# Cross-attention on one core: the turned probabilities moved on two DMA queues, and two score tiles in pairs of 64 rows

## The reference

```python
# B = 8, C1 = C2 = 512, N = 1024, D = 64
q = einsum('bcn,dc->bnd', x1, Wq) + bq
k = einsum('bcn,dc->bdn', x2, Wk) + bk[:, None]
v = einsum('bcn,dc->bdn', x2, Wv) + bv[:, None]
attn = softmax(einsum('bnd,bdm->bnm', q, k), axis=2)
out = einsum('bcm,bnm->bcn', v, attn) + x1
```

## Time and profile before

| | |
|---|---|
| runs | 634.26, 635.60, 635.65 us; median 635.6 |
| profiled execution | 635.0 us, span 633.2 us |
| mean granted TensorE clock | 1.000 |
| TensorE busy | 629.5 us (99%) |
| VectorE, ScalarE, GpSimd busy | 442.9, 328.2, 143.3 us |
| DMA | 102.05 MB, mean 161 GB/s |
| issues of `pt_raw<-blocks` | 240, all on SyncE's queue, 2.3 us each to landing |

### The profile page before, as it was taken

The page is one execution under the profiler, slowest core; times in us unless marked ns, Lnnn a source line. Parts: engine busy times, 40 slices in busy tenths (PEclk is TensorE's granted clock), DMA queues, the critical chain, the costliest instruction groups (busy, mean ns, idle before and its releaser), DMA issues.

```text
span 633.2 us, 13435 instructions
## 1 busy us (share of the span) xinstructions
PE 629.5 (99%) x5318; PEld 590.1 (93%) x5318; DVE 442.9 (70%) x511; ACT 328.2 (52%) x430; POOL 143.3 (23%) x115
## 2 busy tenths in 40 slices
PE   9999999999999999999999999999999999999998
PEld 7888899999999999999999999999999999999986
DVE  6995768847778477794777947778568776597351
ACT  6786535735457345474454653555626547265120
POOL 0332200631007400083000830016300353004100
PEclk9999999999999999999999999999999999999999
DMA  8633426963269532776328762287533974345442
GB/s 334 215 133 83 128 84 181 331 143 111 73 176 324 133 126 82 187 285 166 99 83 204 281 159 89 100 227 260 137 93 114 248 243 114 99 132 133 109 145 81
DMA packets 42758, 102.05 MB, mean 161 GB/s; under 512 B 8176, under 2 KB 10224, under 8 KB 42736
## 3 DMA queue, kind: packets, MB, share of 16 engines
q1 hardware_dynamic: 42736, 101.75, 53.4%
HBM read 51.64 MB, written 16.78 MB: 108 GB/s over the span
## 4 chain that ended last, share of the span: by engine, by line
PE 94%; ACT 2%; SPq 2%; DMA 1%; DVE 1%; issue 0%
PE acc_ps L1158 48%; PE acc_ps L1115 23%; PE s_ps L1080 5%; PE s_ps L1228 4%; PE s_ps L1215 3%; PE acc_ps L1178 3%; PE acc_ps L1353 2%; SPq L298 2%; PE acc_ps L1338 1%; PE s_ps L1082 1%; ACT pt_raw L546 1%; PE acc_ps L1190 1%; PE s_ps L1329 1%; DMA pt_raw<-in_front_dram 1%; ACT pt_raw L552 0%; ACT xs_hi L465 0%
## 5 line engine op out<-in xcount | busy, mean ns | idle before, releaser
L1158 PE MATMUL acc_ps<-pt_hi,vt_hi 64*128 64x512 f32 x960 | 201.5, 386 | 0.2 <-DVE pt_lo L727 0.2
L1158 PE MATMUL acc_ps<-pt_lo,vt_hi 64*128 64x512 f32 x960 | 201.3, 386 | 0.0
L1158 PE MATMUL acc_ps<-pt_hi,vt_lo 64*128 64x512 f32 x960 | 201.3, 386 | 0.0
L1158 PEld LDWEIGHTS acc_ps<-pt_hi,vt_hi 64*128 64x128 f32 x960 | 104.3, 184 | 6.5 <-issue 0.8
L1158 PEld LDWEIGHTS acc_ps<-pt_lo,vt_hi 64*128 64x128 f32 x960 | 104.3, 184 | 5.8
L1158 PEld LDWEIGHTS acc_ps<-pt_hi,vt_lo 64*128 64x128 f32 x960 | 104.3, 184 | 5.8
L1115 PE MATMUL acc_ps<-wv_lo,xs_hi 64*128 64x512 f32 x448 | 95.8, 390 | 0.0
L1115 PE MATMUL acc_ps<-wv_hi,xs_hi 64*128 64x512 f32 x448 | 94.9, 386 | 0.0
L433 POOL TENSOR_TENSOR vt_lo<-vt_lo,v_part 128x64 fp32r<-128x64 f32 x56 | 21.0, 380 | 322.1 <-DVE vt_lo L727 322.1
L558 ACT ACTIVATE probs<-s_ps,negmax 128x1024 f32<-128x1024 f32 x56 | 62.5, 1117 | 54.9 <-DVE negmax L814 54.4
L814 DVE TENSOR_REDUCE negmax<-s_ps 128x1 f32<-128x1024 f32 x64 | 76.7, 1210 | 19.7 <-PE s_ps L1082 18.9
(11 more groups left out here) (140 smaller groups left out, 879.2 us busy)
## 6 DMA issues: line engine op xcount, KB each, us to landing
pt_raw<-blocks SPq DMA_DIRECT2D x240, 128.0 KB, 2.3
stage<-in_x_dram SPq DMA_DIRECT2D x32, 512.0 KB, 6.3
o_sb<-in_x_dram SPq DMA_DIRECT2D x64, 256.0 KB, 3.1
out_dram<-o_sb SPq DMA_DIRECT2D x63, 256.0 KB, 2.1
stage<-in_ctx_dram SPq DMA_DIRECT2D x28, 512.0 KB, 9.0
pt_raw<-in_front_dram SPq DMA_DIRECT2D x4, 512.0 KB, 5.7
v_part<-sums SPq DMA_DIRECT2D x56, 32.0 KB, 1.8
stage<-in_front_dram SPq DMA_DIRECT2D x2, 512.0 KB, 7.6
```

Of the source, the lines that this page charges most:

```text
L1158: mm = nc.tensor.matmul(acc_ps[:, OUT_BANK[group], :], v[rows, m, group * P:(group + 1) * P], p[rows, m, :], start=(swap == 0 and m == 0 a ...
```

## The change

Two things are changed. First, `move` is split: SyncE issues the transfers of steps 0 and 1, ScalarE those of steps 2 and 3, eight each. ScalarE's `move(b, 0)` stands at the head of `v_phase(b)`, its `move(b, 1)` behind the roundings of the next x in `batch(b)`. Both wait for `s_blk` as SyncE's do. Second, score tiles 2 and 3 of the first batch are made by `scores_rows`. For this GpSimd copies columns 256 to 511 of Q's high and low part to `q_dup`, and TensorE waits for the copies.

```diff
+SP_STEPS = (0, 1)
+ACT_STEPS = (2, 3)
...
@@ sync, move
                 sp.wait_ge(s_blk, half_of(b, h) * NT + NT)
-                for step in range(NQ):
+                for step in SP_STEPS:
                     for i in range(NQ):
                         j = (i + step) % NQ
                         sp.dma_start(pt_raw[j * Q:(j + 1) * Q, i, :, :],
...
@@ gpsimd
             pool.wait_ge(s_qlo_a, 1)
             first_x1_lo_b(2)
             first_x1_lo_b(3)
+            pool.wait_ge(s_x1lo_e, 2)
+            pool.wait_ge(s_x1lo_o, 2)
+            pool.wait_ge(s_qhi_a, 1)
+            nc.gpsimd.tensor_copy(q_dup[D:2 * D, QH:NH], q_st[0:D, QH:NH].bitcast(F32)).then_inc(s_qdup_a, 1)
+            pool.wait_ge(s_qdup_a, 1)
+            nc.gpsimd.tensor_copy(q_dup[0:D, QH:NH], q_st[D:2 * D, QH:NH].bitcast(F32)).then_inc(s_qdup_a, 1)
+            pool.wait_ge(s_qdup_a, 2)
...
@@ scalar
+            def move(b, h):
+
+                act.wait_ge(s_blk, half_of(b, h) * NT + NT)
+                for step in ACT_STEPS:
+                    for i in range(NQ):
+                        j = (i + step) % NQ
+                        nc.scalar.dma_start(pt_raw[j * Q:(j + 1) * Q, i, :, :],
+                                     blocks[i * Q:(i + 1) * Q, j, :, :, :].rearrange("p m t r -> p m (t r)")
+                                     ).then_inc(s_moved, 16)
+
             def v_phase(b):
+                move(b, 0)
                 exp(b, 4)
                 exp(b, 5)
...
                         round_x1(nb, 3)
+                move(b, 1)
                 if not last:
                     q_cross(nb, first)
...
@@ tensor
-            scores_next(0, 2)
-            scores_next(0, 3)
+            pe.wait_ge(s_qdup_a, 2)
+            scores_next_rows(0, 2)
+            scores_next_rows(0, 3)
```

More of the change, by code:

```diff
@@ L214, in build @@
         s_acc = sem("s_acc")
+        s_qdup_a = sem("s_qdup_a")
         s_qdup_b = sem("s_qdup_b")
@@ L1102, in scores_next_rows @@
                 scores_rows(t)
-            def scores_next(b, t):
-                pe.wait_ge(s_exp, b * ST + t - 1)
-                scores(t)
             def v_rows(m, swap, k):
```

## The result

| | before | after |
|---|---|---|
| median | 634.86 us (634.26 to 635.65, 5 runs) | 675.11 us (672.63 to 676.14, 5 runs) |
| ratio, with 95% interval | | 1.0623 [1.0598, 1.0648] |
| profiled execution, span | 635.0 us, 633.2 us | 676.1 us, 674.3 us |
| mean granted TensorE clock | 1.000 | 0.974 |

The account below looks back on a forecast made before the run. TensorE, busy 629.5 of 633.2 us, was taken as the bound. From 635.0 us, +5.1 (ScalarE's issues), -0.33 (SyncE's relief) and 0 (score tiles) gave 639.8, raised to 640.1 us; range 634.4 to 652.

Parts of the forecast that it names:

- What bounds the kernel: TensorE, busy 629.5 of 633.2 us; another engine matters only where it is late for TensorE.
- Part 1: First batch's score tiles 2 and 3: two slots saved, 0.45 us, turn into a wait for VectorE's sum; 0 us.
- the bound of 29.9: First batch: GpSimd's two copies to `q_dup`, priced as twice-as-wide ones, end at 29.9, before TensorE wants them at 30.62.
- Part 2: SyncE makes 8 issues, not 16; last rows land about 5 us earlier, batch 0's `pt_lo` gap goes: 0.33 us gained once.
- part 3: ScalarE's eight issues ahead of exp(4) make score tile 6 0.73 us late, seven times: +5.1 us; `move(b, 1)` is free.
- the price of an issue: ScalarE's issues priced by SyncE's same transfer, 0.591 us, pitch 0.63 us: eight take 5.0 us.
- Rival B: Two queues hinder each other; in full, one issue shuts out the other, tile 6 5.8 us late, 680 us; chance 0.22.
- partial form: Queues hinder each other about half as much: pitch 0.9, stall 2.9 us, 655 us; half of the 0.22.
- Rival A: ScalarE's issues are cheap, pitch 0.37, all hidden ahead of tile 6: 634.7 us, or 634.2; chance 0.23.

Follow-up runs that it names:

- the kernel with the same target: Against the kernel after, ScalarE's source order became 2, 3, 0, 1: nth transfers read opposite halves, write the same target block; 656.1 us, ratio 1.0351.
- the kernel with opposite halves: Against the kernel after, SyncE moves source blocks 0 and 1, ScalarE 2 and 3: nth transfers read and write opposite halves; 648.5 us, ratio 1.0211.

## Why the prediction was wrong, step by step

**What bounds the kernel**: right. TensorE does, and only where another engine is late for it. All of the loss is in the matmul starts.

**Part 1, the tiles, 0 us**: right. VectorE's sum and the turn behind it in the kernel after, and GpSimd's two copies:

```profile
28.00 0.39 POOL L419 CAST q_dup<-q_st 64x256 fp32r<-64x256 f32 x1
28.46 0.40 POOL L421 CAST q_dup<-q_st 64x256 fp32r<-64x256 f32 x1
...
31.46 0.74 DVE L763 SCALAR_TENSOR_TENSOR sums<-acc_ps,bias_q,sums 64x512 f32<-64x512 f32 x1 [0.43 <-ACT sums L475]
...
32.35 1.07 PE L1340 MATMUL acc_ps<-ident,blocks 128*128 128x128 f32 x8 [0.16 <-DVE sums L763]
```

The copies end at 28.86, a us ahead of the bound of 29.9. The turn starts behind the sum, 0.15 us after its end, as before; it starts 0.18 us earlier, as the last Q product does (30.21 against 30.39). From start to start less a slot TensorE waits 0.33 us where about 0.4 was forecast; the 0.16 in the row counts from the end that the profile gives the last score matmul.

**Part 2 and batch 0, -0.33 us**: wrong, +2.2 us and a stretch of low clock. The prediction reckoned ScalarE's issues of this `move(0, 1)` at 5.0 us, 55.14 to 60.2, 0.3 us late for `q_cross`. ScalarE in the kernel after, then VectorE and TensorE:

```profile
54.96 7.81 ACTq L600 DMA_DIRECT2D pt_raw<-blocks  x8
62.81 1.02 ACT L475 ACTIVATE sums<-s_ps 64x1024 f32<-64x1024 f32 x1 [8.30 <-issue]
...
69.15 3.88 ACT L475 ACTIVATE pt_hi<-pt_raw 128x1024 fp32r<-128x1024 f32 x4
...
70.85 4.62 DVE L749 TENSOR_TENSOR pt_lo<-pt_raw,pt_hi 128x1024 fp32r<-128x1024 f32 x4
...
72.21 0.50 PE L1175 MATMUL acc_ps<-pt_hi,vt_hi 64*128 64x512 f32 x2 [2.31 <-DVE pt_lo L749]
```

`q_cross` starts 2.88 us later than in the earlier trace rows. What follows it on ScalarE keeps its distances, and the idle 1.43 us ahead of `pt_hi` is used up, so `pt_hi` is 1.36 us late.

The premise of the gain failed for the same reason as part 3. The last rows of a move were to land about 5 us earlier. By the landings in the traces they came 10.89 us after the first issue, where it was 11.75 us before (medians of the moves): 0.9 us earlier, not 5, since two queues together moved only a fifth more per microsecond (204 and 246 GB/s in the windows shown here). The waits of the earlier trace rows also say less than the prediction read in them. Of ScalarE's 31.8 us, 17.5 are one wait in the last batch, which the trace of the kernel after has too (16.6 us, now put down to TensorE); the other eight, 14.3 us, are gone mostly because ScalarE arrives later. And ScalarE was not the only one that waited for the moves: VectorE's turns did, 6.6 us in seven times before. Of all this only the 0.2 us for `pt_lo` in batch 0 reached TensorE.

With four issues on ScalarE the slack is enough. The wait of 0.2 us for `pt_lo` in the earlier trace rows (0.7 us in the kernel with the tiles only) is gone as predicted. The profiled span is 0.3 us shorter, which is less than the runs of one kernel differ by.

**Part 3, +5.1 us**: its chain was right and its price was wrong. The step that failed is *the price of an issue*. It took the pitch of 0.63 us from a queue that was alone and called it the very same transfer. Alone it is that (0.61 us). But the change makes two queues move the blocks at the same time, and in that state it is 0.97. The argument that went with it, that the price hangs on the kind of transfer and not on its size, held for a queue alone (0.59 us for 32 and for 128 KB) and not for two: 0.61, 0.67 and 0.97 us with a quarter, three quarters and all of the bytes. Put the measured 7.75 us into the prediction's own formula, and the stall is 3.5 us instead of 0.73, seven times 24.3; the starts say 23.6. There was a row of before that should have been asked for, the DMA engines during the move (columns as in the windows above):

```profile
258.00:268.00 10.00, 10.00 (x94) 9.53 (x92) 6.64 (x11) 4.51 (x8) 0.97 (x3) 1.00 0.91 204
```

With one queue they were already busy 0.91 of the time, at 204 GB/s; with two it became 0.98 at 246 GB/s. The mean of 161 GB/s of the whole run, which looks like ample room, says nothing of this stretch. A doubled rate of issue had almost nowhere to go.

**A term was missing**: the low clock, 14.6 us, more than a third of the loss. The prediction priced a stall by its length alone. That is right for short ones (below), but not for these.

**Rival B, the two queues hinder each other**: right that they do, and its 680 us in full stands near the measured 675 us by luck. Its stall was 5.8 us, the measured one 3.1 to 3.7; the low clock, which it did not have, filled the difference. Its partial form, a pitch of 0.9 and 655 us, had the stall (2.9 us) nearly right. Its mechanism, that one issue shuts out the other for its whole length, did not hold: with a quarter of the bytes both queues issue at the lone price but for the one collision of 0.26 us. Its argument against the full form, that a wide load's issue takes 0.33 us, spoke to that mechanism and not to the traffic. It had 0.22, and should have had most of the chance once the 0.91 was read, since what it needed was only a pitch of 0.9, by whatever way. The Trainium skill's page "Perfetto Trace Analysis", section "DMA Instruction — HWDGE (DVE, Sync)", says that the descriptor generator is locked for one instruction at a time and that the wait for the lock is part of an issue's length. The runs agree in part: the collision of 0.26 us may be such a wait, but with both queues issuing the medians were 0.59 and 0.61 us, so such a wait alone, without the traffic, does not give 0.97 us.

**Rival A, cheap issues**: no. Every issue on ScalarE took at least 0.51 us.

**What is left open.** The runs show that the issue's length hangs on the bytes and on the order of the transfers in the two queues. That it is the source partitions of the nth pair that matter is the reading that fits the order of all of them; but several transfers of each queue are in flight at once (4 us to landing against less than 1 us per issue), and no run looked at one pair alone. They also don't show how the traffic reaches back to the issuing sequencer: over a step that the two queues share and that the traffic stretches, or in each queue by itself. The Trainium skill says in "SBUF — State Buffer", section "Door 1: The DMA port swizzle (why `[64,N]` ≈ `[32,N]`)", that the first 64 partitions reach one half of the ports and the last 64 the other. The table is in line with that as far as opposite halves on both sides hinder least (0.68 us). But the page makes no difference between source and target, and here there is a large one: 0.70 us with only the sources in opposite halves, 0.97 us with only the targets. The page speaks of the transfer's bandwidth; that the length of an issue follows, only these runs show.

## What to carry to other kernels

A DMA issue on an engine that computes is work on that engine, and its price in the profile is that of the traffic it ran in: before a second queue is added, read the busy share of the DMA engines in that very stretch, and where it is near 0.9 take the price as unknown upwards. Count what fits between the event that releases the issues and the work behind them (here 4.28 us), and give the computing engine no more than fits at the contended price: four issues here, not eight. Where two queues move blocks at the same time, try an order in which they read from different halves of the partitions: here it took back 26.6 of 40.1 us, though four issues were still better.

## What the runs showed of the hardware

- An issue of this transfer (32 partitions, 4 KB each, SBUF to SBUF) takes 0.59 us on SyncE and 0.61 us on ScalarE when only one queue makes them, and the same with both when each moves 1 KB rows. With 4 KB rows on both it grew to 0.97 us on ScalarE where the nth transfers read the same partitions, and to 0.68 us where they read and wrote in opposite halves. Landing grew from 2.3 us to between 4.0 and 4.7 us in every order.
- When both queues' second issues began within 0.01 us of each other, ScalarE's took about 0.87 us instead of 0.61, with 1 KB rows as with 4 KB.
- exp(4) started 0.17 to 0.18 us behind ScalarE's last issue, `q_cross` in batch 0 only 0.04 us.
- The clock. All stalls in the steady loop are given from start to start, less a slot. Those of up to 1.90 us, in all kernels, left it at 1.00; of the three between 1.94 and 2.22 us, all in the kernel with the same target, two were followed by the lower level and the longest was not; from 2.30 us on all were in the profiled executions. The length of the stall does not settle it: of the ten runs of the kernel that shares only `move(b, 1)`, whose one stall was 2.52 us in the profiled run, five have a mean clock of 1.000. The first row below (windows view) is the stretch behind a stall of 1.66 us in the kernel with opposite halves. The second is behind the one stall of the kernel that shares only `move(b, 1)`, of 2.52 us, where slots of 0.43 us cost another 1.53 us.

```profile
506.29:509.69 3.40, 3.40 (x30) 2.92 (x32) 3.19 (x7) 2.02 (x4) 0.42 (x2) 1.00 1.04 290
```

```profile
73.00:76.40 3.40, 3.40 (x20) 3.25 (x22) 3.40 (x4) 1.87 (x2) 0.00 (x0) 0.62 0.00 0
```
